# The end of a quantized layer and the router behind it: two tiles copied on another engine, other PSUM banks, logits ranked in three parts

## The reference

```python
x = x + L0_ffn(cond0(x))   # 32 small experts and a shared one
x = x + L1_ffn(cond1(x))   # two matmuls on values quantized to 8 bits, GELU between
x = x + L2_ffn(cond2(x))   # 8 experts, each token goes to its best 2
x = x + L3_ffn(cond3(x))   # ternary weights

def cond(x):               # gain comes from the side input by two scans
    return sigmoid(x) * gain * (0.8 + 0.2 * tf)

def L1_ffn(c):             # per token: absmax, round to 127 levels, matmul, scale back
    h = gelu(int8_matmul(quant(c), quant(W1)) + B1)     # 256 -> 1024
    return int8_matmul(quant(h), quant(W2)) + B2        # 1024 -> 256
```

## Time and profile before

| | |
|---|---|
| median of 3 runs | 472.86 us (471.51 to 472.87) |
| the profiled execution | 470.68 us, its span 468.9 us |
| busy: PE, DVE, ACT, POOL | 86%, 73%, 50%, 51% of the span |
| mean granted TensorE clock | 0.969 |
| stage of the second layer and the router | about 199 to 264 us of the span |

### The profile page before, as it was taken

One profiled execution on the slowest core, in us unless ns is written; L12 is line 12 of the kernel. 1 busy time (PEld: TensorE's weight loads), 2 busy tenths in 40 slices (PEclk: granted clock), 3 DMA queues, 4 the chain that ended last, 5 costly groups with the idle time before them and its releaser, 6 DMA issues.

```text
span 468.9 us, 5896 instructions
## 1 busy us (share of the span) xinstructions
PE 405.2 (86%) x1678; PEld 257.2 (55%) x1685; DVE 341.3 (73%) x619; ACT 235.2 (50%) x471; POOL 239.6 (51%) x336
## 2 busy tenths in 40 slices
PE   2577999999999999958784899999999999986794
PEld 1466678755455555625562355556666555653553
DVE  5999887999999999789967367547646511028995
ACT  4600276176667766647886323233233233329884
POOL 6544142578778997224000556775775464214641
PEclk9998999999999999976997799999999999999999
DMA  7900000645565645000011798899899986050001
GB/s 228 398 6 0 1 2 30 228 173 176 189 213 192 218 163 207 18 1 1 2 63 37 247 400 301 287 361 330 290 336 349 309 281 257 24 190 0 13 34 47
DMA packets 23664, 77.39 MB, mean 165 GB/s; under 512 B 3440, under 2 KB 7920, under 8 KB 20176
## 3 DMA queue, kind: packets, MB, share of 16 engines
q1 hardware_dynamic: 20336, 69.94, 41.8%
q0 software_dynamic: 2208, 6.03, 4.0%
q10 hardware_dynamic: 1088, 1.05, 0.7%
HBM read 71.76 MB, written 5.24 MB: 164 GB/s over the span
## 4 chain that ended last, share of the span: by engine, by line
PE 34%; issue 5%; DVE 4%; ACT 4%; DMA 3%; POOL 1%; POOLq 0%; ACTq 0%; DVEq 0%
PE bank L1887 17%; PE bank L1907 10%; PE bank L1898 2%; DVE gl L1495 2%; PE bank L1870 1%; DVE pt L1502 1%; ACT q2T L811 1%; PE bank L1763 1%; PE bank L1744 1%; DMA xb<-cond_rows,row_i 1%; PE bank L1941 1%; DMA gy<-y_rows 1%; DMA cond_rows<-cond 1%; PE bank L1755 1%; POOL st L606 1%
## 5 line engine op out<-in xcount | busy, mean ns | idle before, releaser
L1887 PE MATMUL bank<-gu,xbT 128*128 128x512 f32 x184 | 83.2, 595 | 0.9 <-ACT xbT L876 0.9
L1674 PE MATMUL bank<-hx,w2raw 128*128 128x512 f32 x128 | 67.3, 607 | 4.6 <-DVE hx L1230 3.8
L1431 DVE TENSOR_TENSOR hm<-bank,sl 128x512 f32<-128x512 f32 x23 | 15.9, 692 | 67.2 <-issue 31.1
L756 ACT ACTIVATE rl<-bank 128x512 f32<-128x512 f32 x64 | 38.0, 594 | 40.0 <-PE bank L1538 39.2
L1887 PEld LDWEIGHTS bank<-gu,xbT 128*128 128x128 f32 x184 | 34.5, 190 | 35.6 <-issue 33.3
L542 POOL DMA_INDIRECT xb<-cond_rows,row_i x23 | 26.1, 1133 | 49.9 <-DVE row_i L1381 36.5
L1536 PE MATMUL bank<-xlhi,w1hi 128*128 128x512 f32 x64 | 49.3, 771 | 0.0
L1907 PE MATMUL bank<-dn,hT 128*128 128x256 f32 x184 | 45.2, 388 | 3.4 <-ACT hT L887 0.7
L1230 DVE TENSOR_TENSOR hx<-bank,cwb 128x512 f32<-128x512 f32 x64 | 42.2, 661 | 4.8 <-ACT bank L760 4.7
L467 POOL TENSOR_TENSOR fw<-fw,bw 128x256 f32<-128x256 f32 x32 | 24.0, 750 | 41.8 <-DVE bw L1034 41.4
L549 POOL DMA_INDIRECT y_rows<-yb,dest_i x23 | 25.1, 1089 | 35.5 <-ACT yb L893 34.5
(11 more groups left out here) (294 smaller groups left out, 911.8 us busy)
## 6 DMA issues: line engine op xcount, KB each, us to landing
gu<-in_gu SPq DMA_DIRECT2D x22, 1024.0 KB
cwb<-cw_rows SPq DMA_DIRECT2D x32, 512.0 KB, 4.2
dn<-in_dn SPq DMA_DIRECT2D x23, 512.0 KB, 4.6
traw<-in_t SPq DMA_DIRECT2D x3, 1024.0 KB
w1raw<-in_w SPq DMA_DIRECT2D x8, 256.0 KB, 4.9
w2raw<-in_w SPq DMA_DIRECT2D x8, 256.0 KB, 4.5
kT<-in_kt SPq DMA_DIRECT2D x4, 256.0 KB, 4.9
x<-in_x SPq DMA_DIRECT2D x2, 512.0 KB, 7.0
```

What stands on the lines that cost most here:

```text
L756: act.activation(rl[:, u % 3, :], bank[u % 4][:], ACT.Relu).then_inc(sem("r_ready"), 1)
L1674: pe.matmul(bank[4 + s][:], w2raw[:, e // 4 % 2, e % 4, :], hx[:, 0, u % 4, :], start=(e == 0), stop=(e == E0 - 1), skip_group_check=True) ...
L1887: ins = pe.matmul(bank[2 * (b % 2) + up][:], xbT[:, b % 2, k, :], gu[:, b % RING, k, up * I2:up * I2 + I2], start=(k == 0), stop=(k == KC ...
```

## The change

It has five parts.

1. The fourth gain of the second layer moves to bank 5, and the third part of the first layer's latent output to bank 2; `turn_gain(1, 3)` moves behind `turn_rows(1)`, and `l1_up(1)` waits for `x1_ready` 3 in place of `cond_ready` 8. ACT's `l1_first(1)` comes ahead of a table load.
2. `second` writes bank 4 for tiles 5 and 7; for tiles 5 to 7 its wait for `l1_out` is looser (none for 5, tile 4's for 6, tile 5's for 7). The scales' small buffer `pt` has four slots, and DVE takes `l1_scales(7)` before `l1_out(4)`.
3. For tiles 6 and 7 DVE copies the turned hidden values (`l1_last`), not ACT; so ACT loads the sigmoid table right after `l1_quant(7)`. PE turns both tiles before it multiplies either, and takes `turn_gain(2, b)` earlier, in pieces. `euk3` is formed on POOL.
4. `cond2_bank`, the order of ACT's `cond_turned` and `sigmoid_pair(2, 3)` and the order on PE of `logits_up`, `turn_cond2` and `logits_back` change.
5. The router's logits are ranked in three parts of 4, 2 and 2 tiles (`RANKED`) in banks 7, 4 and 3.

```diff
-ROUTED = {"mk": 2, "lsub": 3, "slab": 4, "rows": 5, "dest": 6, "weights": 8}
+ROUTED = {"mk": 3, "lsub": 4, "slab": 5, "rows": 6, "dest": 7, "weights": 9}
+LAST = 2
-LOGITS = {"up": [1, 2, 4, 5], "back": [3, 6]}
+LOGITS = {"up": [1, 2, 4, 5], "back": [3, 6, 7]}
+RANKED = [(0, 4, 7), (4, 2, 4), (6, 2, 3)]
...
-            return bank[((0, 1, 1, 7), (0, 1, 6, 2), (0, 1, 2, 3), (0, 2, 1, 3))[l][b]]
+            return bank[((0, 1, 1, 7), (0, 1, 6, 5), (0, 1, 2, 3), (0, 2, 1, 3))[l][b]]
...
+        def second_bank(t, tag):
+            return bank[4 if not tag and t in (5, 7) else 7][:, 0:C]
+
+        def logits_bank(t):
+            first, count, b = RANKED[0 if t < TH else t // 2 - 1]
+            return bank[b][:, (t - first) * E2:(t - first) * E2 + E2]
...
-            return bank[(4, 6, 5, 7)[v]]
+            return bank[(4, 6, 2, 7)[v]]
...
+            for i in range(NBLK):
+                pool.tensor_scalar(euk3[:, i, :], kT[:, i, :], ubk[:, 3, i // KC, i % KC:i % KC + 1], 30.0, ALU.add, ALU.min
+                                   ).then_inc(sem("kup3_ready"), 1)
...
+            l1_first(1)
             load_table(1, ACT.Gelu_apprx_tanh)
-            l1_first(1)
...
-                if t == NT - 1:
-                    load_table(6, ACT.Sigmoid)
-                l1_second(t)
+                if t < NT - LAST:
+                    l1_second(t)
...
+            load_table(6, ACT.Sigmoid)
...
+            def l1_last(t):
+                wait(dve, sem("m2_ready"), t - 1)
+                for h in range(2):
+                    dve.wait_ge(sem("q2t_ready"), 2 * t + h + 1)
+                    dve.tensor_scalar(q2T[:, t % 2, 4 * h:4 * h + 4, :], bank[5 + h][:].rearrange("p (c n) -> p c n", n=P), -ROUND, None, ALU.add
+                                      ).then_inc(sem("q2T_last"), 1)
...
-            for s in range(2):
-                t = slice(TH * s, TH * s + TH)
+            for s, (first, tiles, b) in enumerate(RANKED):
+                t = slice(first, first + tiles)
...
             turn_gain(1, 2)
-            turn_gain(1, 3)
...
             turn_rows(1, "", "q1_ready")
-            pe.wait_ge(sem("cond_ready"), 8)
+            turn_gain(1, 3)
+            pe.wait_ge(sem("x1_ready"), 3)
...
             def second(t, tag, out_ready, weight):
-                wait(pe, sem(out_ready), t)
+                if tag or t < NT - 3:
+                    wait(pe, sem(out_ready), t)
+                elif t >= NT - LAST:
+                    pe.wait_ge(sem(out_ready), t - 1)
...
             logits_up(0)
+            logits_up(1)
             turn_cond2(2)
-            logits_up(1)
-            turn_cond2(3)
+            pe.wait_ge(sem("x2_ready"), NT)
             logits_back(0)
             logits_back(1)
+            turn_cond2(3)
```

More of the change, by code:

```diff
@@ L1313, in _ @@
             l1_pre(2)
[L1314 to L1316 removed]
+            def l1_last(t):
[4 more added lines that the diff above has]
+                                      ).then_inc(sem("q2T_last"), 1)
+            for t in range(NT - 2):
+                l1_scales(t + 1)
                 if t + 3 < NT:
                     l1_pre(t + 3)
+                if t == NT - 3:
+                    l1_scales(NT - 1)
                 if t >= 1:
                     l1_out(t - 1)
[L1321 to L1324 removed]
+            l1_out(NT - 3)
+            l1_last(NT - 2)
+            l1_last(NT - 1)
             make_cond(2, 0)
             make_cond(2, 1)
+            l1_out(NT - 2)
             l1_out(NT - 1)
@@ L1331, in _ @@
             make_cond(2, 3)
-            lg = [bank[i][:, 0:TH * E2].rearrange("p (t e) -> p t e", e=E2) for i in (7, 5)]
             def per_token(i):
@@ L1751, in turn_hidden @@
                 for h in range(2):
-                    wait(pe, sem("q2T_ready"), 2 * (TILES[tag] + t) - 1 + h)
+                    if not tag and t == NT - 1:
+                        pe.wait_ge(sem("q2T_last"), h + 1)
+                    else:
+                        wait(pe, sem("q2T_ready"), 2 * (COPIED[tag] + t) - 1 + h)
                     for j in range(4):
@@ L1758, in second @@
             def second(t, tag, out_ready, weight):
-                wait(pe, sem(out_ready), t)
+                if tag or t < NT - 3:
+                    wait(pe, sem(out_ready), t)
+                elif t >= NT - LAST:
+                    pe.wait_ge(sem(out_ready), t - 1)
                 for c in range(8):
-                    if c % 4 == 0:
-                        pe.wait_ge(sem("q2T_ready"), 2 * (TILES[tag] + t) + c // 4 + 1)
-                    ins = pe.matmul(bank[7][:, 0:C], q2T[:, t % 2, c, :], weight(c), start=(c == 0), stop=(c == 7))
+                    if c % 4 == 0 and not tag and t >= NT - LAST:
+                        pe.wait_ge(sem("q2T_last"), 2 * (t - NT + LAST) + c // 4 + 1)
+                    elif c % 4 == 0:
+                        pe.wait_ge(sem("q2T_ready"), 2 * (COPIED[tag] + t) + c // 4 + 1)
+                    ins = pe.matmul(second_bank(t, tag), q2T[:, t % 2, c, :], weight(c), start=(c == 0), stop=(c == 7))
                 ins.then_inc(sem("m2_ready"), 1)
@@ L1780, in _, with l1_down @@
             pe.wait_ge(sem("x1_ready"), 4)
-            for t in range(NT):
+            pe.wait_ge(sem("cond_ready"), 8)
+            def l1_down(t):
+                second(t, "", "x2_ready", lambda c: q2w[:, c, :])
+            for t in range(4):
                 turn_hidden(t, "", "q2_ready")
-                if t + 4 < NT:
-                    turn_rows(t + 4, "", "q1_ready")
-                if t == NT - 2:
-                    pe.wait_ge(sem("pre_ready"), NT)
-                    for b in range(B):
-                        turn_gain(2, b)
-                second(t, "", "x2_ready", lambda c: q2w[:, c, :])
-                if t + 4 < NT:
-                    l1_up(t + 4)
+                turn_rows(t + 4, "", "q1_ready")
+                l1_down(t)
+                l1_up(t + 4)
+            turn_hidden(4, "", "q2_ready")
+            pe.wait_ge(sem("pre_ready"), NT - 1)
+            turn_gain(2, 0)
+            turn_gain(2, 1)
+            l1_down(4)
+            turn_hidden(5, "", "q2_ready")
+            pe.wait_ge(sem("pre_ready"), NT)
+            turn_gain(2, 2)
+            l1_down(5)
+            turn_gain(2, 3)
+            turn_hidden(6, "", "q2_ready")
+            turn_hidden(7, "", "q2_ready")
+            l1_down(6)
+            l1_down(7)
             def turn_cond2(b):
```

40 lines of the change are left out of this document (18 added, 22 removed).

## The result

| | before | changed |
|---|---|---|
| median | 472.87 us (4 runs, 471.51 to 473.18) | 468.48 us (4 runs, 467.38 to 469.69) |
| ratio, 95% interval | | 0.992 [0.9893, 0.9947] |
| the profiled execution, its span | 470.68, 468.9 us | 467.98, 466.1 us |
| mean granted clock | 0.969 | 0.967 |

The account below looks back on a forecast made before the run. It took the serial stage up to the router's marks as the bound. Start, end and ranking put the marks at 248.8 against 253.06, −4.3 us: 466.4 profiled, 468.6 from the median, given as 468.4 us, range 466.2 to 470.8.

Parts of the forecast that it names:

- What bounds: Serial stage through the router: gathers and weights' fetch hang on it, so sooner marks move the rest as a block.
- Start, −2.0: Second layer's start: `l1_up(1)` no longer waits for the last `make_cond`, so `l1_pre(1)` starts 1.99 us sooner.
- rival 4: First tiles: PE's clock stays high at the start, DVE's short waits vanish; −4.8 to −5.3 us, chance 0.06.
- Rival 2: First tiles: PE's low clock takes back up to 1.5 us of the start's gain; −2.8 us, chance 0.12.
- End, −2.5 more: Tiles 6 and 7 to first ranking: DVE's copies and earlier sigmoids bring the ranking sooner; headed −2.5 us.
- Rival 3: Layer's end: the copies cost more than they save, last output 0.8 us later; −3.5 us, chance 0.10.
- Ranking, +1.3: Router's ranking: three parts spend 6.3 us where 4.99 were, the split costing about 0.5.
- `euk3` on POOL, 0: Moving eight instructions from DVE to POOL gains nothing by itself; at most 6.0 us, covered by POOL's idle time.
- The sum: Instruction behind the last marks at 248.8 in place of 253.06, −4.3 us; 468.4 us on the runs' footing.

Follow-up runs that it names:

- start_only: The kernel before with part 1 of the change alone; ratio 0.9995 [0.9969, 1.0021].
- euk_dve: The changed kernel with the eight `euk3` instructions back on DVE, behind its copies; ratio to before 0.9972 [0.9944, 1.0001].
- start_warm: start_only with 18 matmuls that nobody reads in PE's idle stretches at the second layer's start; ratio to before 0.9962 [0.9939, 0.9985].
- two_parts: The changed kernel with the logits ranked in two parts of four tiles, the second in bank 4; ratio to before 0.9903 [0.9876, 0.9931].
- changed_again: The changed kernel as it is, run and traced once more; ratio to before 0.9892 [0.9848, 0.9936].
- start_again: The same kernel as start_only, run once more; ratio to before 0.997 [0.9946, 0.9994].
- start_busy: start_warm with further matmuls that nobody reads around the router, the same as in before_busy; ratio to before 0.9972 [0.9942, 1.0001].
- end_only: The changed kernel with part 1 undone; ratio to before 0.9963 [0.9934, 0.9993].
- two_busy: two_parts with start_warm's unread matmuls at the second layer's start and before_busy's around the router; ratio to before 0.9884 [0.9843, 0.9926].
- before_busy: The kernel before with PE kept busy around the router by matmuls that nobody reads; ratio to before 1.0007 [0.9977, 1.0036].

## Why the prediction was right, point by point

Counted from the first quantization, then put on the clock of before (1.44 us off each time of after):

| step | forecast | measured |
|---|---|---|
| `l1_up(1)` starts | 203.0 | 202.90 |
| `l1_pre(1)` starts | 205.9 | 205.85 |
| output 3 | 229.92 | 229.50 |
| sigmoids | 236.7 | 236.21 |
| last of tile 7's copies ends | 237.3 | 237.43 |
| first ranking copy | 242.5 | 242.50 |
| second part, third part | 245.2, 247.0 | 245.06, 246.85 |
| behind the marks | 248.8 | 248.64 |
| gathers | 255.8 | 255.58 |

- **What bounds.** Right. Gathers and blocks followed the marks as a block: from the first block to the span's end 204.02 and 204.04 us.
- **Start, −2.0.** Right in mechanism, small in size: −2.05 at `l1_pre(1)`, but −2.41 from tile 0's output on. The 0.35 more is the 0.25 us wait ahead of `l1_pre(4)`, which fell away because PE was at full clock for longer; I had counted that as rival 4 alone (and wrote that DVE has no idle time long enough to matter behind 205.91). start_only has −2.36 by itself. Rival 2 was seen in one of the eleven traces that have the new start (euk_dve), with 1.06 us of its 1.5, and start_warm shows that otherwise the low clock takes nothing.
- **End, −2.5 more.** This figure over the paragraph fits no sum of the prediction: its steps give −3.6 up to the first ranking copy, −2.3 with the ranking, and −2.0 − 2.3 is the −4.3 that it forecast. I go by the steps. Their sum is right (−5.57 at the first ranking copy, −5.6 forecast), with two terms off that cancel: 0.35 too little from the start, and so −3.16 here for −3.6 to that point. The copies took 1.29 us a pair, 0.69 each and 0.60 apart, within 0.6 to 0.75. Tile 7's waited 0.28 us for PE and its own turning 0.51 for them, so they ended 0.55 later than the shifted output 3 allowed. Rival 3 was right in kind, at 0.4 us in place of 0.8, and was paid for by the start's surplus: that the two errors are of one size is luck. Out of a bank, 128 x 512 costs the copy about what it costs the product (659 ns after, before). The Trainium skill says on the page VectorE: DVE Perf Modes, section "Why PSUM operands drop a tier", that with an operand in PSUM a float32 instruction has no fast mode. The traces agree in direction: the eight `euk3` of euk_dve, of SBUF operands, took 2.18 us for twice the elements of such a pair of copies (2048 against 1024 a partition), which took 1.29. The same copy out of SBUF, which would show it alone, is in no run.
- **Ranking, +1.3.** Measured 6.14 us where 6.3 was forecast: half part instructions of 0.28 to 0.29 as interpolated, and a wait of 0.08 for 0.2 ahead of the second part. The split's cost of 0.5 is 0.57 in two_parts.
- **`euk3` on POOL, 0.** Right for the sum, since POOL idled 24.63 us more before the gathers; wrong in two ways beside it. I named 6.0 us as its upper bound from rows of 750 ns; it took 9.77. The right row was there in the kernel before: a group of POOL's sixteen instructions of the same form (`eu` from `kT` and a column, line 445) at 1178 ns each. And "leaving it gains nothing by itself" holds in the old order only: in the new one the place where it stood is no longer idle, and euk_dve lost 3.4 us by it. Of the contention between DVE and POOL that the prediction weighed nothing shows: while `euk3` ran (222.6 to 232.4) DVE's absmax took 1.21 us and the small scale instructions 0.14 to 0.21, as before 222.
- **The sum.** −4.42 against −4.3 in the stretch. The medians moved by 4.4, those of changed_again by 4.9, and the mean differences are 4.1 (standard error 0.6) and 4.6 (0.6). That 468.48 came within 0.1 us of 468.4 is luck on top of a right sum: four runs with a spread of 2.3 us don't fix a median so well. The time forecast for a profiled execution, 466.4, was 1.6 too low (467.98), 1.44 of it the late start.

**What stays open.** The parts' gains in time fall short of their gains in the traces. Over start_only and start_again the mean gain is about 1.2 us (standard error 0.35) for 2.4 in the stretch, and start_warm and start_busy, which have the same part, gained 1.7 and 1.3; end_only's is 1.7 (0.6) for 2.4. The whole change gives 4.1 to 4.6 for 4.4. The traces show how that can be: the rest behind the first block is 204 us in seven of the fourteen traces and 205 to 208 in the others, and in all seven of these the clock had fallen again (5.40 for 3.70 us in start_again's first block; 0.66 in 460 to 465 us in start_again and two_busy, 1.00 there before and after; 0.66 in 420 to 425 in before_busy, which has the old start). If the shorter start made such falls more frequent, that would be the missing 1.2 us; one trace a run can't show how often they come. The mean granted clock, which is on record for every run, leans that way without showing it. In the windows from 202 to 220 us, clock times time falls short of full speed by 6.8 us in before and by 3.4 in start_only and start_again, so that, as an estimate, their mean clock should be higher by 0.007. Over their 24 runs it is higher by 0.001 (0.002). The base is weak: end_only, with the old start, has 1.7 us there. before_busy against start_busy is a gain of 1.9 (0.7), between the two; but the clock was not held all the way to the block in either (0.59 in 262 to 265, and 0.68 in 256 to 259). That is not settled.

No version clearly beats the changed kernel. By its trace two_parts should, by 0.57 us, and its two ratios (0.9903 and, with dummy matmuls, 0.9884) do not contradict it; 0.57 us is 0.12%, below what these runs tell apart.

## What to carry to other kernels

Find the one serial stage that everything behind it hangs on, follow a single engine through it, and add up that engine's own waits: the sum held to 0.2 us although two of its terms were off. Price a moved operation by a row of the same engine, form and operands, not of a similar size; and ask once more, in the new order, what each neighbour hides, because a move worth nothing alone (`euk3`, the second bank) can be what the rest needs. Where executions differ by more than the gain, count both traces from an instruction ahead of all that the change can shorten, and let the runs say what the whole change is worth.

## What the runs showed of the hardware

- POOL's `tensor_scalar` of 128 x 256 float32 took 1.14 us with a column added and then a minimum with a number, and 0.48 us for the quantization of the same size (L530: times a column, plus a number). At one size the two operations make a factor of 2.4.
- Identical instruction lists ran from 469.8 to 476.5 us in the runs of before (93 runs on three chips). In the traces such microseconds go with PE's granted clock: 12 to 24 us (0.62 to 0.64, or 1.00, with 1.2 to 3.1 us between the two groups at the first quantization), the first blocks, 410 to 425 us, and 455 to 465 us. All but the first blocks lie far from the edited instructions.
- PE's clock fell to half behind a rest of 1.94 us in euk_dve, and made 2.1 us of delay into 3.4; behind rests of 1.88 and 1.38 us at the changed kernel's start it fell as well, and cost nothing, because DVE was the slower engine there.
